# A sandwich of linear attention and expert feed-forward on one core: where the K stabiliser, the norm weights, the V bias and the row norm are computed, the order on TensorE and ScalarE, and the layout of the selection's one-hots

## The reference, cut to what matters

```python
def softmax_kernel(x, proj, is_query):
    norm, ratio = x.shape[-1] ** (-0.25), proj.shape[0] ** (-0.5)
    xp = einsum('bhnd,md->bhnm', x * norm, proj)
    diag = sum(square(x), -1, keepdims=True) * 0.5 * norm * norm
    stab = max(xp, -1) if is_query else max(xp, (-1, -2))   # per row / per head
    return ratio * (exp(xp - diag - stab) + 1e-4)
...
q, k, v = (split(video @ W.T + b) for W, b in ((Wq, bq), (Wk, bk), (Wv, bv)))
qp, kp = softmax_kernel(q, proj, True), softmax_kernel(k, proj, False)
denom = einsum('bhnm,bhm->bhn', qp, sum(kp, 2))
out = einsum('bhnm,bhmd->bhnd', qp, einsum('bhnm,bhnd->bhmd', kp, v)) / denom
x = layer_norm(video + out @ Wo.T + bo, g2, be2)
ff = relu(x @ W1.T + b1) @ W2.T + b2
return layer_norm(x + ff, g3, be3)
...
x = x + layernorm(attention(layernorm(x)))          # x1
xf = layernorm(x)
scores = softmax(xf @ gate_w.T); vals, idx = top_k(scores.T, 512)
y = layernorm(xf[idx]) * ln_w + ln_b                # per expert
h = gelu(y @ fc1.T + b1); out = (h @ fc2.T + b2) * vals
x = x + layernorm(xf.at[idx].add(out))
```

## Time and profile before

| | us |
|---|---|
| median of 3 runs | 1052.07 (1051.35 to 1055.75) |
| the profiled execution, its own time | 1056.98 |
| its span | 1055.2 |
| start to the first key projection | 13.39 |
| eight bodies with attention, 13.39 to 628.10 | 614.7 |
| two trailing bodies, to the first step of the search at 709.57 | 81.5 |
| search and one-hots, to the first gather's indices at 786.73 | 77.2 |
| experts and last stage | 268.5 |

### The profile page before, as it was taken

The page is one execution under the profiler, slowest core; times in us unless marked ns, Lnnn a source line. Parts: engine busy times, 40 slices in busy tenths (PEclk is TensorE's granted clock), DMA queues, the critical chain, the costliest instruction groups (busy, mean ns, idle before and its releaser), DMA issues.

```text
span 1055.2 us, 15181 instructions
## 1 busy us (share of the span) xinstructions
PE 782.8 (74%) x5501; PEld 590.3 (56%) x5501; DVE 654.7 (62%) x1522; ACT 371.2 (35%) x530; POOL 418.4 (40%) x340
## 2 busy tenths in 40 slices
PE   5368898998898898898998877421116999999920
PEld 3236656666575566566666656321115888889820
DVE  2536427658658658658668565668883665667535
ACT  1434434534534524524524612000004434344314
POOL 4151323344533534534534524220062444444247
PEclk9678899999999999998999997855556999999975
DMA  6000010002011011011010010112004565554165
GB/s 206 1 21 1 1 41 1 10 32 61 21 38 43 20 40 40 20 40 40 20 40 22 20 57 24 60 63 84 0 5 156 154 161 155 139 136 127 26 165 174
DMA packets 60602, 65.01 MB, mean 62 GB/s; under 512 B 7952, under 2 KB 57232, under 8 KB 60560
## 3 DMA queue, kind: packets, MB, share of 16 engines
q1 hardware_dynamic: 53584, 55.63, 16.3%
q0 software_dynamic: 6144, 8.52, 4.6%
q10 hardware_dynamic: 832, 0.30, 0.1%
HBM read 43.33 MB, written 21.10 MB: 61 GB/s over the span
## 4 chain that ended last, share of the span: by engine, by line
PE 48%; DVE 24%; issue 12%; POOL 6%; DMA 5%; ACT 4%; POOLq 0%; DVEq 0%; ACTq 0%; SPq 0%
PE pF L1393 12%; PE pX L1599 9%; PE pX L1423 5%; DMA xg<-row_scratch,idx_g 4%; PE pA L1337 3%; PE pX L1351 3%; PE pA L1403 3%; PE pA L1322 3%; DVE st L834 3%; DVE qe L1083 3%; DVE mxk L865 2%; PE pF L1351 2%; POOL xg L766 2%; PE pF L1436 2%; PE pA L1344 1%
## 5 line engine op out<-in xcount | busy, mean ns | idle before, releaser
L1393 PE MATMUL pF<-w,h 128*128 128x256 f32 x512 | 125.9, 403 | 14.1 <-ACT h L471 14.1
L1393 PEld LDWEIGHTS pF<-w,h 128*128 128x128 f32 x512 | 100.9, 202 | 36.7 <-ACT h L471 15.7
L774 POOL DMA_INDIRECT acc_scratch<-at,idx_s x32 | 51.7, 1614 | 106.9 <-DVE at L1185 100.2
L1351 PE MATMUL pF<-x2T_hi,w_lo 128*128 128x512 f32 x128 | 61.2, 478 | 29.8 <-DVE x2T_lo L938 21.3
L599 ACT ACTIVATE h<-pX,b1cur 128x512 f32<-128x512 f32 x64 | 44.1, 690 | 100.5 <-PE pX L1351 39.0
L694 POOL TENSOR_SCALAR ve<-mv 128x4 f32<-128x4 f32 x48 | 11.3, 236 | 167.9 <-DVE mv L838 147.6
L1599 PE MATMUL pX<-w_lo,h_hi 128*128 128x256 f32 x256 | 74.3, 290 | 0.8 <-issue 0.8
L1599 PE MATMUL pX<-w_hi,h_lo 128*128 128x256 f32 x256 | 73.4, 287 | 0.0
L1599 PE MATMUL pX<-w_hi,h_hi 128*128 128x256 f32 x256 | 73.2, 286 | 0.0
L844 DVE TENSOR_SCALAR z<-z,mv,rstd 128x256 f32<-128x256 f32 x64 | 48.5, 818 | 37.5 <-POOL rstd L696 37.5
L1168 DVE TENSOR_TENSOR h_lo<-h,h_hi 128x512 fp32r<-128x512 f32 x64 | 42.9, 690 | 30.4 <-ACT h_hi L591 26.9
(11 more groups left out here) (249 smaller groups left out, 2007.4 us busy)
## 6 DMA issues: line engine op xcount, KB each, us to landing
kp<-fc1T SPq DMA_DIRECT2D x8, 1024.0 KB
w<-fc2T SPq DMA_DIRECT2D x8, 1024.0 KB
xin<-video SPq DMA_DIRECT2D x8, 512.0 KB, 3.7
x<-video SPq DMA_DIRECT2D x8, 512.0 KB, 4.5
x_scratch<-x SPq DMA_DIRECT2D x8, 512.0 KB, 2.9
acc_scratch<-xf SPq DMA_DIRECT2D x8, 512.0 KB, 2.9
row_scratch<-y SPq DMA_DIRECT2D x8, 512.0 KB, 3.0
qp<-x_scratch SPq DMA_DIRECT2D x2, 1024.0 KB
```

The source lines that it names most:

```text
L774: pool.indirect_dma_start(acc_d, bass.IndirectOffsetOnAxis(ap=idx_s[:, g:g + 1], axis=0), og[:, g, :], None, compute_op=ALU.add).then_inc( ...
L1351: ins = nc.tensor.matmul(dst[:], w_[:, k, tok(n)], x_[:, k, :], start=(m == 0), stop=(m == len(parts) - 1))
L1393: ins = nc.tensor.matmul(slots[m][:, half * D:(half + 1) * D], h[:, k, tok(2 * m + half)], w2[:, k, :], start=(k == 0), stop=(k == FC - 1))
```

## The change

It has these parts.

1. The maximum over partitions of K's features: `kmax` is turned on TensorE (`turn_kmax`), reduced by VectorE from PSUM (`k_top`), put on a diagonal and spread over the partitions by a second matmul with ones (`spread_kmax`). VectorE now subtracts kbias from all four tiles.
2. g2 is multiplied into W1's rows before its split, and be2 @ W1 is added to b1 (`fold_ready`, `bias_ready`), so x2 is turned right after its normalisation. The residual still needs x2 * g2 + be2 + b2: GpSimd does it in two steps behind.
3. bv is folded: bv @ Wo is added to bo, and V leaves PSUM on ScalarE as a copy.
4. y: the row norm's root comes from x1's variance v (1 / sqrt(v (1 + eps) + eps^2)), so y is made from x1 on ScalarE (`normed_rows`), and stats, root and normalisation number 5 go. ln_w and ln_b are applied to the turned rows of each expert, by token column, in `turned`.
5. The order on TensorE and ScalarE in a body.
6. The one-hots: 4 groups in place of 8, digits outside and tokens inside, float16 in all operands, the id product on VectorE, and one masked product for `Rbd`.

```diff
 # TensorE
+                def turn_kmax():
+                    pe.wait_ge(kmax_ready, i + 1)
+                    nc.tensor.transpose(slot_a(i, J_ST)[0:H, 0:P], kmax[:], ident[:]).then_inc(a_ready, 1)
+                def spread_kmax():
+                    pe.wait_ge(stab_ready, i + 1)
+                    nc.tensor.matmul(slot_a(i, J_ST + 1)[:, 0:H], ones_h[:], sdiag[:], start=True, stop=True).then_inc(a_ready, 1)
...
                 if ff:
-                    pe.wait_ge(x2_ready, f + 1)
-                    for c in range(C):
-                        turn_tokens(slot_f(f, u, "f", J_X2T + c), x2, c).then_inc(f_ready, 1)
+                    pe.wait_ge(x2l_ready, (f + 1) * C)
+                    if isinstance(f, int) and f == 0:
+                        pe.wait_ge(w1_split, C + 2)
+                    hidden(0)
+                    hidden(1)
                 if att:
                     features(i, J_XK + 1, kT, 1)
                     pe.wait_ge(qT_ready, (i + 1) * G)
+                    if isinstance(i, int) and i == 0:
...
+                            ins = nc.tensor.matmul(pF[1][:, 0:D], bv_wide[:, c], wo[:, c, :], start=(c == 0), stop=(c == C - 1))
...
+                if isinstance(i, int) and i == 0:
...
+                    for n in range(FC):
+                        for c in range(C):
+                            ins = nc.tensor.matmul(pF[0][:, n:n + 1], w1_raw[:, c, tok(n)], be2_c[:, c:c + 1], start=(c == 0), stop=(c == C - 1))
+                    ins.then_inc(fold_ready, 1)
 # ScalarE
+            def normed_rows(u):
+                act.wait_ge(x1_ready, u + 1)
+                act.wait_ge(ny_ready, u + 1)
+                wait(act, y_out, 16 * u)
+                for t in range(TT):
+                    ins = nc.scalar.activation(y[:, t, :], x1[:, t, :], ACT.Identity, bias=ny[:, t:t + 1], scale=ry[:, t:t + 1])
+                ins.then_inc(y_ready, 1)
...
-                    nc.scalar.activation(xgT_hi[:, c, :], pM[c], ACT.Copy).then_inc(xgT_ready, 1)
+                    wait(act, xgl_ready, (e - 1) * C + c + 1)
+                    nc.scalar.activation(xga[:, c, :], pM[c], ACT.Identity, bias=lnb_c[:, c:c + 1], scale=lnw_c[:, c:c + 1]).then_inc(xga_ready, 1)
+                    act.wait_ge(xga_ready, e * C + c + 1)
+                    nc.scalar.activation(xgT_hi[:, c, :], xga[:, c, :], ACT.Copy).then_inc(xgT_ready, 1)
 # GpSimd
-                    nc.gpsimd.partition_all_reduce(stabk[:], kmax[:], P, RMAX).then_inc(stab_ready, 1)
...
+                    pool.wait_ge(f_ready, f * F_JOBS + J_X2T + 2)
+                    nc.gpsimd.tensor_tensor(x2[:], x2[:], g2_b[:].unsqueeze(1).to_broadcast([P, TT, D]), ALU.mult).then_inc(x2b_ready, 1)
...
-                    pool.wait_ge(w1_in, 16)
+                    pool.wait_ge(wff_in, 16 * N_WFF)
+                    pool.wait_ge(fold_ready, 2)
+                    for c in range(C):
+                        nc.gpsimd.tensor_scalar(w1_raw[:, c], w1_raw[:, c], g2_c[:, c:c + 1], None, ALU.mult).then_inc(w1_split, 1)
 # VectorE
-                    sf.link(nc.vector.tensor_tensor(x2[:], x2[:], over_tiles(g2_b), ALU.mult))
-                    nc.vector.tensor_tensor(x2[:], x2[:], over_tiles(be2_b), ALU.add).then_inc(x2_ready, 1)
...
+            def k_top(i, steps):
+                dve.wait_ge(a_ready, i * A_JOBS + J_ST + 1)
+                steps.link(nc.vector.tensor_reduce(smax[:], pA[J_ST % 2][0:H, 0:P], AX_X, ALU.max))
+                nc.vector.tensor_scalar(sdiag[:], ident[0:H, 0:H], smax[:, 0:1], None, ALU.mult).then_inc(stab_ready, 1)
...
+            for k in range(2):
+                for c in range(C):
+                    n += 1
+                    one_hot(oneB, dig_b, k, c, SB).then_inc(oneb_ready, 1)
+                    one_hot(oneA, dig_a, k, c, SA).then_inc(onea_ready, 1)
+                    dve.wait_ge(oneb_ready, n)
+                    nc.vector.tensor_tensor(oneB[:, k, :, :, c].rearrange("p b e s -> p (b e) s"), oneB[:, k, :, :, c].rearrange("p b e s -> p (b e) s"),
+                                            idval[:, c].unsqueeze(1).to_broadcast([P, 4 * SB, SEG]), ALU.mult).then_inc(onehot_ready, 1)
```

More of the change, by code:

```diff
@@ L229, in build @@
         Rbd = sb("Rbd", [P, 2, 4, SB], F16)
+        Rbd_be = Rbd[:].rearrange("p k e b -> p k b e")
         idm = sb("idm", [P, E, SR, GT])
@@ L906, in body @@
                     stats(1, sf, r)
+                    sf.end()
                 if u is not None:
@@ L929, in body @@
                         nc.vector.tensor_tensor(z[:], z[:], over_tiles(be3_b), ALU.add).then_inc(za_ready, 1)
+                if f is not None:
+                    for c in range(C):
+                        dve.wait_ge(x2T_ready, f * C + c + 1)
+                        nc.vector.tensor_tensor(x2T_lo[:, c, :], pF[c][:], x2T_hi[:, c, :].bitcast(F32), ALU.subtract).then_inc(x2l_ready, 1)
                 if i is not None:
@@ L934, in body @@
                     norms(i, 1, dgk)
-                if f is not None:
-                    for c in range(C):
-                        dve.wait_ge(x2T_ready, f * C + c + 1)
-                        nc.vector.tensor_tensor(x2T_lo[:, c, :], pF[c][:], x2T_hi[:, c, :].bitcast(F32), ALU.subtract).then_inc(x2l_ready, 1)
+                if u is not None:
+                    dve.wait_ge(za_ready, u + 1)
+                    stats(3, su, z)
                 if i is not None:
@@ new lines, in _, with one_hot @@
+            done.link(nc.vector.tensor_copy(dig_b.rearrange("p e c s -> p c e s"), digi_b))
+            def one_hot(dst, digit, k, c, size):
+                return nc.vector.tensor_tensor(dst[:, k, :, :, c], digit[:, 4 * k:4 * k + 4, c].unsqueeze(1).to_broadcast([P, size, 4, SEG]),
+                                               iotah[:, 0:size].unsqueeze(2).to_broadcast([P, size, 4, SEG]), ALU.is_equal)
+            n = 0
+            for k in range(2):
+                for c in range(C):
+                    n += 1
+                    one_hot(oneB, dig_b, k, c, SB).then_inc(oneb_ready, 1)
[3 more added lines that the diff above has]
+                                            idval[:, c].unsqueeze(1).to_broadcast([P, 4 * SB, SEG]), ALU.mult).then_inc(onehot_ready, 1)
@@ L1136, in _ @@
             dve.wait_ge(ids_ready, 1)
-            for k in range(2):
-                for q in range(4):
-                    ins = nc.vector.tensor_copy(Rbd[SA * q:SA * q + SA, k, q, :], pX[0][SA * q:SA * q + SA, k, SB * q:SB * (q + 1)])
-            ins.then_inc(rbd_ready, 1)
+            nc.vector.tensor_tensor(Rbd_be, pX[0][:, :, 0:4 * SB].rearrange("p k (b e) -> p k b e", e=4),
+                                    rmask[:].unsqueeze(1).unsqueeze(1).to_broadcast([P, 2, SB, 4]), ALU.mult).then_inc(rbd_ready, 1)
@@ L1530, in body @@
                 if att:
-                    turn_out(2)
-                    turn_out(3)
+                    pe.wait_ge(oT_ready, (i + 1) * 3)
+                    for t in range(TT):
+                        turn_out(t)
                 if gt_:
@@ L1574, in _ @@
             n = 0
-            for c in range(C):
-                for s0 in range(0, SEG, 4):
+            for k in range(2):
+                for c in range(C):
                     n += 1
@@ L1579, in _ @@
                     pe.wait_ge(onehot_ready, n)
-                    for s_ in range(s0, s0 + 4):
-                        first, final = n == 1 and s_ == 0, c == C - 1 and s_ == SEG - 1
-                        for k in range(2):
-                            ins = nc.tensor.matmul(pX[0][:, k, 0:4 * SB], oneA[:, c, s_, 4 * k:4 * k + 4, :].rearrange("p e a -> p (e a)"),
-                                                   oneB[:, c, s_, 4 * k:4 * k + 4].rearrange("p e b -> p (e b)"), start=first, stop=final)
+                    for s_ in range(SEG):
+                        ins = nc.tensor.matmul(pX[0][:, k, 0:4 * SB], oneA[:, k, :, :, c, s_].rearrange("p a e -> p (a e)"),
+                                               oneB[:, k, :, :, c, s_].rearrange("p b e -> p (b e)"),
+                                               start=(c == 0 and s_ == 0), stop=(c == C - 1 and s_ == SEG - 1))
             ins.then_inc(ids_ready, 1)
```

298 lines of the change are left out of this document (152 added, 146 removed).

## The result

The changed kernel takes 970.93 us (median of four runs, 968.63 to 971.5) where the kernel before takes 1052.11: a ratio of 0.922, 95% interval 0.919 to 0.924, so it is faster by 81 us. The forecast was 978, with a range from 963 to 998.

| stretch | before | after | gained | forecast |
|---|---|---|---|---|
| start | 13.39 | 13.83 | -0.4 | 0 |
| body 0 | 74.82 | 63.61 | 11.2 | 3.6 |
| body 1 | 75.77 | 74.84 | 0.9 | 7.3 |
| five full bodies | 387.12 | 339.72 | 47.4 | 36.5 |
| the body behind them | 77.00 | 67.10 | 9.9 | 7.8 |

The account below looks back on a forecast made before the run. TensorE was taken to set the pace of the eight batches, losing time to waits and its lower clock. Savings 36.5 + 7.8 + 7.3 + 3.6 + 8.8 + 11.6 - 1.2 = 74.4 gave 982.6, with the median 4.9 lower 978; range 963 to 998.

Parts of the forecast that it names:

- The wait for oT: Full bodies: ScalarE makes y ahead of oT, so the third attention product waits 1.3 us.
- that for at: Full bodies: the four turns of oT stand together, without work between them to hide VectorE's divisions: 0.8 us.
- the second features product: Full bodies: it needs the first query exponential (1.88 us), covered by 1.8 of context matmuls: 0.3 with the semaphore.
- its two operations: Full bodies: x2's two VectorE operations over 128x1024 go, some 1.2 us each; x2T_lo's wait of 3.4 us goes.
- 5 for the maximum: Body 0: the maximum over TensorE saves some 5 us in the chain to the context, where nothing covers it.
- The folded matmuls: Body 0: 16 one-column matmuls and two of 256 for the folded biases cost 5.5 us in all.
- my upper bound of 4.7: Body 1: W1's two scalings bounded at 1.9 and 4.7 us; x2 2.3 to 5.0 late, 2.8 taken.
- Two of the signs: Changed profile: granted clock at its upper level from the second body on; wrong if TensorE waits over 5 us a body.
- Rival 1: One-hots stay at one element a cycle: 8.4 us more, 986; chance 0.12.
- Rival 2: Bodies: VectorE's subtractions wait at the port shared with GpSimd: 12 to 20 us, 990 to 998; chance 0.22.
- Rival 3: Bodies come closer to 66.7 us because y and the divisions fit: 2.1 less in seven, 963; chance 0.13.
- Rival 4: Kernel ends slower: ScalarE's y ahead of oT comes more than 12 us later than 53.1; chance 0.03.

Follow-up runs that it names:

- experiment 2: Changed kernel with two VectorE operations (times g2, plus be2) put back behind x2's normalisation, the place of its turns kept: 975.11 us, ratio 0.923.
- Experiment 3: Changed kernel with the maximum over partitions reduced on GpSimd again, without TensorE's two small matmuls and VectorE's two small steps: 996.03 us, ratio 0.944.
- the unchanged ones: Seven profiles, the changed kernel's among them, that leave body 0 as it is; their second body starts at 77.4 to 79.7.
- experiments 6 to 8: Changed kernel, folded matmuls early in body 0: W1's scalings on VectorE 964.67 us, on GpSimd 964.50; spread over three gaps, W1 split on VectorE, 960.29.
- experiment 5: Changed kernel with the two tables of the one-hots in four bytes instead of two: 979.47 us, ratio 0.928.
- experiments 6 and 7: Changed kernel, folded matmuls moved behind the maximum's spread in body 0; W1's scalings on VectorE (964.67 us) or on GpSimd (964.50 us).

## Why the prediction was right, and where its terms were not

**Full bodies: mechanism right, 2.1 us a body too little.** Forecast 70.1, measured 67.96. Of the difference 1.2 is TensorE's busy time: I counted 3.1 us of clock where it fell by 3.85 (69.73 to 65.88) with 0.4 of new matmuls in it. The other 0.9 is its idle time, 2.1 instead of 3.0. The wait for oT is 0.8 instead of 1.3, because y begins 1.1 earlier; that for at 0.5 instead of 0.8; the second features product waits for nothing (0.3); small gaps are 0.2 longer. What I wrote of x2, that its two operations "go" and its turns follow at once, is two things. I priced the operations at 1.2 us each by their shape, where the second took 3.26 in that very body, and experiment 2 shows that in the new order they are worth nothing. How the 3.38 us divide between them, V and the place of the turns stays open.

**Body 0, forecast 3.6, measured 11.2.** From the first query features to the first attention product the chain is 6.8 us shorter (32.10 to 66.17 before, 32.34 to 59.57 after), where I had counted 5 for the maximum. Experiment 3 puts the reduction back and its second body starts at 80.7, 2.5 behind the median of the unchanged ones (which scatter by 2.3 themselves); the other 4 us come from the rest of the chain, by the timelines GpSimd's two subtractions and ScalarE's order, which I had costed at nothing there. That split is argued, not shown; the two were not undone by themselves. The denominators' product is 4.0 nearer to the first one (4.1 forecast). Behind it, without the folded matmuls, the body's end takes 12.4 us instead of 16.1, because the clock is at its upper level there (0.74 before and 1.00 after, for the windows from 60 on): the wait that had held the product up is gone, and behind it the product itself takes 1.92 us instead of 3.64. The folded matmuls took 3.6, not 5.5. The profile after has the fastest body 0: the median of the seven is 65.0 us long, not 63.6, so some 1.3 of the 11.2 are scatter.

**Body 1, forecast 7.3, measured 0.9.** The term that was mis-sized is W1's preparation on GpSimd and what follows from it. Two scalings by a column take 5.68 us, above my upper bound of 4.7: I had bounded them by a product of two full operands, and they are slower than that. So x2 comes 4.0 us late instead of 2.8, and behind the folded matmuls and behind that wait the clock is low (key projection 5.38 instead of 3.60, x2's turns 1.97 instead of 1.04), which I had not counted. With both out of the way the body takes 66.4 (experiments 6 to 8); I had forecast 65.7 without x2's delay. Two of the signs that I had named fail in this body: the clock is granted at 0.93, not at its upper level, and TensorE idles for 7.0 us, more than 5.

The two errors, 7.6 too little and 6.4 too much, nearly cancel, and that was luck. What is left is on one side: the full bodies and the one behind them gave 13.0 us more than forecast. By the profiles the stages gave 86.6 us where I had 74.4; by the medians, 81.2.

**The rest.** The trailing bodies gave 9.2 (8.8 forecast). The one-hots' round is 2.35 (2.4 forecast), but the last sixteen matmuls take 2.15 instead of 1.2, which was named as a bound. The experts and the last stage take 2.1 more instead of 1.2: 1.3 is TensorE's wait for the first expert's turned rows (2.82 us instead of 1.50), behind ScalarE's two operations more; the other 0.8 was not followed up.

**Rivals.** Rival 1 did not come, and experiment 5 shows its size. Rival 2's meetings are in every full body (7.68 to 7.81 us for z), not on the subtractions it named but on an operation that has slack; where the slack was missing (experiments 6 and 7) one cost 3 to 4 us. Rival 3 has the full bodies' size, 2.1 less, but its reason, that y and the divisions fit, is 0.8 of it. Rival 4 did not come: y was early.

**Not undone by themselves** were V's move to ScalarE, the norm number 5 that went, GpSimd's lighter queue and the trailing bodies' parts: for these the gain is read from the timelines.

## What to carry to other kernels

A wait on TensorE of 3 us cost 5 here, since the clock fell behind it: price waits with the clock, from a stretch without any. Ask of each late operand whether its work or its place in the queue makes it late, and undo one at a time. What an undone part costs holds for the new order; what it was worth in the old one only a run from the old kernel shows. Price an operation by its own row, not by its shape: the addition of 1.2 us took 3.26 where another engine met it. Before one-off preparation is moved into a gap, look at the gap's clock and at what stands behind each engine that the work will block.

## What was not expected of the hardware

- Thirty-two one-column float32 instructions take 3.63 us with the clock at 1.00 and 6.99 at 0.50, and the key projection that followed them without a gap ran at 0.68 (77.44 to 82.80).
- VectorE's normalisation of four times 256 elements, one tensor input and two columns, took 7.6 to 8.5 us beside GpSimd's copy and subtraction of 128x2048 and 7.7 to 7.8 beside its sums of 128x1024, instead of 1.4; a product of 128x8 with two SBUF inputs took its usual 0.17 beside GpSimd's scaling by a column, and 4.33 before the change beside its subtraction.
- A float16 matmul whose moving operand is read with a stride of 64 bytes takes twice as long (110 against 54 ns for 64 columns); a stationary operand read so costs a tenth (60 against 54).
- GpSimd's scaling of 128x1024 by a column takes 2.84 us, a product of two such operands 2.4.
